# Router tables in column groups and no stay-awake products between the late ranks and the first expert slot

## The reference

```python
x = x + xattn(layernorm(x), ctx)
x = x + attn(layernorm(x))
h = layernorm(x)
logits = einsum('bsd,ed->bse', h, gate_w) + gate_b        # 8 experts
topv, topi = top_k(logits, 2)                             # the others are set to -inf
gate = softmax(logits)                                    # over the two that are kept
out = x + sum_e gate_e * (h @ expert_w[e] + expert_b[e])
```

## Time and profile before

| What | Value |
|---|---|
| median of 3 runs | 802.32 us (801.78 to 802.72) |
| the profiled execution | 802.31 us, its span 800.5 us |
| busy: TensorE, VectorE, ScalarE, GpSimd | 780.4, 489.1, 340.2, 216.1 us |
| mean granted clock of TensorE | 0.982 |
| cross and self attention | until about 667 us |
| router's end, tables | 667 to 707 us |
| 23 expert slots | 707 to 780 us |
| tail | 780 to 800.5 us |

### The profile page before, as it was taken

One profiled execution on the slowest core, in us unless ns is written; L12 is line 12 of the kernel. 1 busy time (PEld: TensorE's weight loads), 2 busy tenths in 40 slices (PEclk: granted clock), 3 DMA queues, 4 the chain that ended last, 5 costly groups with the idle time before them and its releaser, 6 DMA issues. The chain is left out here.

```text
span 800.5 us, 21117 instructions
## 1 busy us (share of the span) xinstructions
PE 780.4 (97%) x8838; PEld 660.1 (82%) x8839; DVE 489.1 (61%) x1121; ACT 340.2 (42%) x815; POOL 216.1 (27%) x192
## 2 busy tenths in 40 slices
PE   8999999999999999999999999999899998899997
PEld 7888888889888888888988888887677776888884
DVE  6766575566655656457556565757889987522236
ACT  5533534335434354344533445435376653023330
POOL 0222223212232222221332223321232330146630
PEclk9999999999999999999999999999999999589999
DMA  8722001000110001100010001202842328435548
GB/s 286 280 81 80 29 28 54 28 29 29 33 50 28 28 29 46 36 28 29 30 54 28 28 29 28 106 29 84 365 160 112 130 104 302 178 116 171 181 135 301
DMA packets 22443, 78.08 MB, mean 98 GB/s; under 512 B 3248, under 2 KB 3760, under 8 KB 19408
## 3 DMA queue, kind: packets, MB, share of 16 engines
q1 hardware_dynamic: 18672, 64.71, 22.2%
q0 software_dynamic: 3680, 12.06, 4.5%
HBM read 58.15 MB, written 18.61 MB: 96 GB/s over the span
## 5 line engine op out<-in xcount | busy, mean ns | idle before, releaser
L158 PE MATMUL bank<-chi,wparts 128*128 128x258 f32 x496 | 143.7, 290 | 0.0
L160 PE MATMUL bank<-chi,wparts 128*128 128x258 f32 x496 | 140.1, 282 | 0.0
L159 PE MATMUL bank<-clo,wparts 128*128 128x258 f32 x496 | 140.0, 282 | 0.0
L331 POOL TENSOR_TENSOR pdiag_hi<-p_last_and_rinv_hi,const 128x256 fp32r<-128x256 f32 x32 | 19.7, 617 | 328.8 <-DVE p_last_and_rinv_hi L578 328.8
L325 POOL TENSOR_TENSOR ksin<-kb,const 128x1032 f32<-128x1032 f32 x32 | 95.0, 2969 | 40.1 <-ACT kb L378 40.1
L783 PE MATMUL bank<-wparts,chi 128*128 128x512 f32 x256 | 105.8, 413 | 0.0
L158 PEld LDWEIGHTS bank<-chi,wparts 128*128 128x128 f32 x496 | 93.5, 189 | 12.8 <-issue 12.8
L784 PE MATMUL bank<-wparts,chi 128*128 128x512 f32 x256 | 101.3, 396 | 0.0
L785 PE MATMUL bank<-wparts,clo 128*128 128x512 f32 x256 | 101.1, 395 | 0.0
L370 ACT ACTIVATE chi<-craw 128x1032 fp32r<-128x1032 f32 x32 | 34.2, 1069 | 146.4 <-PE bank L785 144.2
L554 DVE TENSOR_TENSOR v<-bank,bias_cross 128x512 f32<-128x512 f32 x64 | 43.8, 687 | 83.9 <-PE bank L785 83.9
(11 more groups left out here) (316 smaller groups left out, 1706.8 us busy)
## 6 DMA issues: line engine op xcount, KB each, us to landing
craw<-ctx_t_dram SPq DMA_DIRECT2D x32, 516.0 KB, 3.5
expert_lo<-weights_dram SPq DMA_DIRECT2D x8, 1024.0 KB, 13.5
expert_hi_scratch<-wraw SPq DMA_DIRECT2D x16, 512.0 KB, 3.0
wparts<-expert_hi_scratch SPq DMA_DIRECT2D x8, 1024.0 KB, 9.3
wraw<-weights_dram SPq DMA_DIRECT2D x7, 1024.0 KB, 5.6
expert_lo<-ffn_out_scratch SPq DMA_DIRECT2D x16, 256.0 KB, 5.1
x<-x_dram SPq DMA_DIRECT2D x8, 256.0 KB, 7.8
ffn_xn_scratch<-xn SPq DMA_DIRECT2D x8, 256.0 KB, 2.3
```

What stands on the lines that cost most here:

```text
L158: pe.matmul(psum, ahi(c), bhi(c), start=(c == 0), stop=False)
L159: pe.matmul(psum, ahi(c), blo(c), start=False, stop=False)
L160: last = pe.matmul(psum, alo(c), bhi(c), start=False, stop=(c == chunks - 1))
```

## The change

Six edits, all on TensorE but the last:

1. The four products of gate_w's column sums and the four of the last tile's logits are issued by narrow instead of whole.
2. Late ranks (of kept_late) are issued by narrow; the early ones stay whole.
3. The urgent table (b_cp) is issued by narrow, four column groups.
4. The gate table (b_v) is issued by a new helper in_halves, two column groups of 64.
5. The three calls of stay_awake between the early ranks and the first slot (1, 2 and 2 products) are gone.
6. In TAIL_ADDS the sums of tiles 0 and 1 are moved ahead of the first adds of tiles 2 and 3.

```diff
-            TAIL_ADDS = ([(t, k) for p in (0, 2) for k in range(2) for t in (p, p + 1)]
-                         + [(0, 3), (1, 3)] + [(t, k) for k in range(2) for t in (4, 5)]
+            TAIL_ADDS = ([(t, k) for k in range(2) for t in (0, 1)] + [(0, 3), (1, 3)]
+                         + [(t, k) for k in range(2) for t in (2, 3)] + [(t, k) for k in range(2) for t in (4, 5)]
...
+                def in_halves(psum, a, b, start, stop):
+                    for q in range(0, P, P // 2):
+                        last = pe.matmul(psum[q:q + P // 2], a[:, q:q + P // 2], b, start=start, stop=stop)
+                    return last
...
                 for c in range(KC):
-                    last = whole(b_q[:, 0:NE], xn[:, 0:P], gate_w[:, c, :], c == 0, c == KC - 1)
+                    last = narrow(b_q[:, 0:NE], xn[:, 0:P], gate_w[:, c, :], c == 0, c == KC - 1)
...
-                    last = whole(b_k[:, 0:NE], x_t_last[:, c * P:(c + 1) * P], gate_w[:, c, :], c == 0, c == KC - 1)
+                    last = narrow(b_k[:, 0:NE], x_t_last[:, c * P:(c + 1) * P], gate_w[:, c, :], c == 0, c == KC - 1)
...
                 for t in range(T - 1):
-                    ranks_behind(t, kept[:, t, :], False)
-                stay_awake(b_v, 1)
+                    ranks_behind(t, kept[:, t, :], False, whole)
                 pe.wait_ge(s_kept, 2)
-                whole(b_score[:, (T - 1) * NE:TILES * NE], rc(R_BEFORE, P), kept_late.rearrange("p t e -> p (t e)"),
+                narrow(b_score[:, (T - 1) * NE:TILES * NE], rc(R_BEFORE, P), kept_late.rearrange("p t e -> p (t e)"),
                        False, False)
-                ranks_behind(T - 1, kept_late[:, 0, :], False)
-                ranks_behind(T, kept_late[:, 1, :], True).then_inc(s_rank, 1)
-                stay_awake(b_v, 2)
+                ranks_behind(T - 1, kept_late[:, 0, :], False, narrow)
+                ranks_behind(T, kept_late[:, 1, :], True, narrow).then_inc(s_rank, 1)
...
-                    last = whole(b_cp[:, 0:SLOTS], at_place[:, j, :], payload[:, j, 0:SLOTS], j == 0, j == K2 - 1)
+                    last = narrow(b_cp[:, 0:SLOTS], at_place[:, j, :], payload[:, j, 0:SLOTS], j == 0, j == K2 - 1)
                 last.then_inc(s_table, 1)
                 pe.wait_ge(s_payload, 2)
                 for j in range(K2):
-                    last = whole(b_v[:, 0:SLOTS], at_place[:, j, :], payload[:, j, SLOTS:2 * SLOTS], j == 0, j == K2 - 1)
+                    last = in_halves(b_v[:, 0:SLOTS], at_place[:, j, :], payload[:, j, SLOTS:2 * SLOTS], j == 0, j == K2 - 1)
                 last.then_inc(s_table, 1)
-                stay_awake(b_score, 2)
```

More of the change, by code:

```diff
@@ L1933, in _, with ranks_behind @@
                 ranks = b_score[:, 0:(TILES + 1) * NE]
-                def ranks_behind(t, kept_t, stop):
+                def ranks_behind(t, kept_t, stop, product):
                     behind = TILES - t
-                    return whole(b_score[:, (t + 1) * NE:(TILES + 1) * NE].rearrange("p (t e) -> p t e", e=NE),
+                    return product(b_score[:, (t + 1) * NE:(TILES + 1) * NE].rearrange("p (t e) -> p t e", e=NE),
                                   rc(R_ONES, P), kept_t.unsqueeze(1).to_broadcast([P, behind, NE]), False, stop)
```

## The result

| | us, median (lowest to highest) | runs |
|---|---|---|
| before | 802.52 (801.78 to 803.01) | 4 |
| after | 792.03 (791.13 to 794.51) | 4 |

The ratio is 0.9875, 95% interval 0.9849 to 0.9901. The changed kernel is faster by about 10 us; the forecast was 792.7 us in a range of 790.7 to 796.5. The profiled execution took 791.18 us, its span is 789.4 us: 11.1 us less than before.

A forecast was written before the change was run, and what follows sets the result against it. TensorE, busy nearly throughout, was taken as the bound, with a chain of short steps before the first expert slot. Gains 1.2 + 1.15 + 4.5 + 3.45 = 10.3, less 1.5, plus 0.85: 802.31 - 9.65 = 792.7 us, range 790.7 to 796.5.

The forecast's parts named there:

- Step 1: Column sums and last logits: four column groups save 0.6 us at each of the two places, together 1.2 us.
- Step 2: Late ranks: in four groups they end before VectorE is ready, so its wait goes, a gain of 1.15 us.
- Step 3: Urgent table: four groups take at most twice their full-clock cost, 3.0 us at half clock; the step gives 4.5 us.
- Step 4: From the tables to slot 0: gate table hidden beside the gather, which waits for the store; the step gives 3.45 us.
- Step 5: Start of slot 0: without the earlier wide work, its products run 3.3 us at half clock, 1.5 us lost.
- rival (a): Slot 0: the clock comes back late, 3.3 us more at half and another 1.5 us lost; 794.2 us, chance 0.18.
- Rival (e): Expert slots: without stay-awake products the clock stays at half through the slots; slower, 803.6 us with 27 us, chance 0.03.
- Step 6: Tail: sums of tiles 0 and 1 fill VectorE's gap, so the last add ends earlier; 0.85 us gained.
- (b): Gate table: two column groups do not overlap, it takes 6.83 us and slot 0 is 1.6 us later; 794.3 us, chance 0.12.
- (d): Urgent and gate tables: small passes cost issue time, so four groups gain nothing at half clock; 798.8 us, chance 0.04.

The follow-up runs named there:

- e7: The changed kernel with the products of the column sums and of the last logits whole again; median 794.69 us, ratio 0.9903 to the kernel before.
- e1: The changed kernel with the old order of the tail adds; median 792.61 us, ratio 0.9887 to the kernel before.
- e4: The changed kernel with only the last stay-awake call back, two products behind the gate table; median 794.02 us, ratio 0.9872 to the kernel before.
- e5: The changed kernel with the gate table whole again; median 793.72 us, ratio 0.9904 to the kernel before.
- e10: The changed kernel with the store of the last tile's normed rows ahead of the loads of experts 6 and 7; median 795.75 us, ratio 0.9900.
- e9: The changed kernel with 21 small products (42 passes) added ahead of the last attention product; median 796.89 us, ratio 0.9924 to the kernel before.
- e3: The changed kernel with the early ranks in four column groups too; median 800.17 us, ratio 0.9942 to the kernel before.
- c0_after_again: The changed kernel itself run again, with no edit; median 796.52 us, ratio 0.9905 to the kernel before.
- e2: The changed kernel with all three stay-awake calls back (1, 2 and 2 products); median 795.79 us, ratio 0.9893 to the kernel before.
- e11: The changed kernel with the last stay-awake call back and the normed rows' store ahead of the loads of experts 6 and 7; 795.99 us, ratio 0.9894.
- e6: The changed kernel with the urgent table whole again; median 795.76 us, ratio 0.9929 to the kernel before.

## Why the prediction was right, point by point

In the profiled execution the sum is 9.08 us where 9.65 was foretold. By the prediction's steps:

| step | foretold | measured |
|---|---|---|
| 1, logits in four groups | 1.2 | 0.65 |
| 2, ranks | 1.15 | 0.31 |
| 3, urgent table | 4.5 | 4.60 |
| 4, tables to slot 0 | 3.45 | 2.86 |
| 5, clock given back | -1.5 | -0.50 |
| 6, tail | 0.85 | 1.16 |

- **Step 1** was right in its durations (e7 shows 1.1 us at L1684), and short by half in this execution: the route constants came 0.39 us too late, a DMA that hangs on the same chain, and the last logits ran at half clock (0.62 instead of 0.37).
- **Step 2 is the step that failed.** It took for granted that the clock would fall where it fell before, at the end of the early ranks. It fell ahead of them, 11.5 us behind t = 0 where it was 14.3 before, the early ranks took 3.18 us instead of 1.91, and VectorE kept 0.87 of its 1.19 us of waiting. In e1, e4, e5 and e10, where the clock fell later, VectorE took the ranks at 14.6 to 14.9 us, and the step gave what was foretold. A part of a kernel in which the clock falls should have been costed at both levels.
- **Step 3** was right, though its price was a guess: 18.4 ns a pass, under twice the 11.6 ns of full clock. VectorE paces it, 2.35 us for 2.49 us of its own work. The two floors of 25 and 62 ns that the Trainium skill gives (TensorE: Matmul & The Clock Gate, Part 1) don't hold for passes in column groups: 128 passes in 2.35 us.
- **Step 4**: the landing of the store was forecast well (690.6 us, against 688.4 + 2.06 = 690.4 on the old scale), but the gather starts 0.9 us behind a landing, not 0.1. As VectorE was late itself, the store did not bind here (0.1 us apart); in e1, e4, e5 and e9 it did. The gate table is hidden, as e5 shows. What was not foretold: gather 0 took 4.65 us and not 3.7, more than the 0.59 us that the step lacks.
- **Step 5** was too dark: slot 0 ran only 1.1 us at half clock, since the clock came back at 697.84. From slot 0's product to the end of the last slot it is 73.76 us against 73.26. In the other variants it came back 0.7 to 2.6 us behind slot 0's first product, in e3 5.7 us behind it: rival (a) is real, though not in the changed kernel's two profiles. Rival (e), the clock at half through the slots, has no support in any of these profiles.
- **Step 6** is right for an execution like the profiled one and too high for others.
- Rivals (b) and (d) fell with 56.6 and 18.4 ns a pass.

The total was nearer than its parts: the losses of steps 1, 2 and 4 (1.98 us) were met by gains of 1.41 us in steps 3, 5 and 6. That is luck, and so is the last half microsecond of the median: 792.03 is 10.5 us below the kernel before, the same kernel in c0_after_again only 7.9, and by their intervals the two gains are 7.9 to 12.1 and 5.5 to 9.8 us. The runs bear out a gain of 8 to 10 us and where it comes from, not 9.65.

## What to carry to other kernels

The float32 products here were paid by the pass and not by the column: a whole pass took 124 ns at full clock with 8 columns (0.99 us for 8) as with 72 (1.74 us for 14 in e4). Splitting one into column groups made it 1.9 (two) and 3.0 times (four, paced by VectorE) shorter at half clock, and this pays where somebody waits for the product. Count instructions before doing it everywhere: the same for the early ranks cost 3.7 us instead of gaining 0.8, 2.5 of it by stops for instructions ahead of slot 0 and the rest with the clock at half through slot 0. And once a step of 5 us is gone, follow every DMA that the old step had covered (here the store, the gathers, the constants), and cost the stage at both levels of the clock.

## What the runs showed of the hardware that was not expected

- TensorE can stop for 1.0 to 2.6 us within a run of like products, at places on a grid of 127 passes (254 instructions with weight loads), and goes on 1.4 us behind the end of an instruction packet of 16 KB.
- The clock's fall to half between attention and experts lay anywhere from 677.4 to 686.0 us in the profiles, and its return from 697.7 to 707.7. Behind t = 0 the fall came at 11.5 to 12.0 us in six profiles and at 14.3 to 18.2 in the eight others, and one and the same program up to there is in both sets (the changed kernel and e4). It was at half for 3.4 us around 42 us in most profiles, for 6.8 us in e2 and not at all in the changed kernel's first profile and in e9, with no edit there. I take this for most of the spread of 3 to 8 us, without having shown it, seen between executions of one kernel.
- ScalarE paused for 4.5 to 5.0 us in one slot, always the same one, in all eight profiles of two chips (groups 1 and 3) and in none of the six others. In e4_awake_last:

```profile
740.13 0.69 ACT L1341 ACTIVATE k_self<-quad,wraw 128x512 f32<-128x512 f32 x1 [4.50 <-remote]
```

It costs TensorE 1.29 to 1.37 us, 0.17% of the time. What causes it is open.
- From the issue of gather 0 to the transposes that wait for it it is 4.78, 4.92 and 5.04 us in the changed kernel, c0_after_again and e11, and 3.61 to 3.76 in e1, e3, e4, e6, e7 and e9. In the first three an instruction packet ran beside the gather's own data (691.07 to 692.43 us in the changed kernel, where that data began to move at 691.26), in the six others none did; in e10 one ran beside gather 1, which was the late one. So the packet is the likely cause of the microsecond that gather 0 took beyond the forecast. This is argued from the times alone; no run moved the packet by itself.
